# Inner attention's P ahead of the second half of its features, its rounded part first, and a new order of turns

## The reference

```
e = leaky_relu(s_i + t_j);  e = where(mask, e, -inf);  out_i = sum_j softmax_j(e)_ij * (h @ W)_j
```

## Time and profile before

| | us |
|---|---|
| median of the runs | 2882.01 |
| the profiled execution's own time | 2880.97 |
| its span, first to last instruction | 2879.2 |
| TensorE matmuls busy | 2827.2 (98%) |
| VectorE busy | 2551.1 (89%) |
| ScalarE busy | 2169.4 (75%) |
| GpSimd busy | 575.6 (20%) |
| mean granted TensorE clock | 0.996 |

### The profile page before, as it was taken

How to read it: one execution, slowest core, us unless ns; L and a number is a source line. 1 busy time by engine, 2 the same in 40 slices (tenths; PEclk the granted TensorE clock), 3 DMA queues, 4 the chain that set the end, 5 groups by cost and what they waited for, 6 DMA issues and landing times. The chain is left out here.

```text
span 2879.2 us, 66889 instructions
## 1 busy us (share of the span) xinstructions
PE 2827.2 (98%) x25368; PEld 2593.7 (90%) x25368; DVE 2551.1 (89%) x7305; ACT 2169.4 (75%) x5791; POOL 575.6 (20%) x731
## 2 busy tenths in 40 slices
PE   7999999999999999999999999999999999999998
PEld 7888998999999999998999999999989998999986
DVE  6898888998999899989988989889899888998977
ACT  5677778777777777787777787777777777777766
POOL 4021022211122211122211222111222111222001
PEclk8999999999999999999999999999999999999999
DMA  2000000000000000000000000000000000000000
GB/s 82 9 10 8 16 16 16 1 16 16 16 16 16 1 16 16 16 16 9 9 16 16 16 16 9 9 16 16 16 16 2 16 16 16 16 16 2 9 8 15
DMA packets 16800, 42.05 MB, mean 15 GB/s; under 512 B 5344, under 2 KB 7392, under 8 KB 16480
## 3 DMA queue, kind: packets, MB, share of 16 engines
q1 hardware_dynamic: 16480, 37.77, 3.7%
HBM read 20.99 MB, written 16.78 MB: 13 GB/s over the span
## 5 line engine op out<-in xcount | busy, mean ns | idle before, releaser
L690 PE MATMUL bank<-hw,R 128*128 128x257 f32 x3072 | 716.5, 381 | 4.4 <-DVE R L905 2.0
L690 PEld LDWEIGHTS bank<-hw,R 128*128 128x128 f32 x3072 | 562.2, 190 | 85.7 <-issue 11.1
L1380 POOL TENSOR_TENSOR rs<-ve,mhalf 128x4 f32<-128x4 f32 x128 | 133.5, 1043 | 1754.7 <-DVE ve L848 1649.5
L905 DVE SCALAR_TENSOR_TENSOR R<-bank,E,mask_ne 128x512 f32<-128x512 f32 x640 | 451.0, 741 | 19.1 <-PE bank L678 16.3
L592 PE MATMUL bank<-wfc_hi,oThi 128*128 128x256 f32 (+1 forms) x1024 | 302.5, 295 | 0.0
L592 PE MATMUL bank<-wfc_hi,oTlo 128*128 128x256 f32 (+1 forms) x1024 | 289.6, 283 | 0.0
L592 PE MATMUL bank<-wfc_lo,oThi 128*128 128x256 f32 (+1 forms) x1024 | 289.6, 283 | 0.0
L724 PEld LDWEIGHTS bank<-hw,R 128*64 128x64 f32 x8192 | 252.2, 139 | 29.3 <-issue 16.7
L724 PE MATMUL bank<-hw,R 128*64 128x65 f32 x8192 | 270.5, 225 | 6.6 <-DVE R L905 4.1
L1197 ACT ACTIVATE Z<-bank,rs 128x258 f32<-128x258 f32 (+1 forms) x384 | 177.8, 477 | 81.1 <-PE bank L592 80.8
L592 PEld LDWEIGHTS bank<-wfc_hi,oThi 128*128 128x128 f32 x1024 | 194.0, 189 | 1.7
(11 more groups left out here) (275 smaller groups left out, 8807.5 us busy)
## 6 DMA issues: line engine op xcount, KB each, us to landing
x<-in_x_dram SPq DMA_DIRECT2D x32, 512.0 KB, 3.5
out_dram<-x SPq DMA_DIRECT2D x31, 512.0 KB, 2.6
R<-in_adj_dram SPq DMA_DIRECT2D x2, 512.0 KB, 7.1
Z<-in_L_gnn_mlp_w_dram SPq DMA_DIRECT2D x2, 512.0 KB, 5.5
O<-in_L_gnn_W_fc_dram SPq DMA_DIRECT2D x1, 1024.0 KB, 6.8
out_dram<-x SPq DMA_DIRECT2D x4, 128.0 KB, 1.7
R<-in_L_gnn_W_dram SPq DMA_DIRECT2D x1, 256.0 KB, 3.8
R<-in_L_gnn_W_hand_dram SPq DMA_DIRECT2D x1, 256.0 KB, 6.6
```

The source lines that it names most:

```text
L690: ins = e.matmul(bk[:, 0:257], P[:, j, i * 128:(i + 1) * 128], hw[:, j, 0:257], start=(j == 0), stop=(j == NBLK - 1))
L905: e.scalar_tensor_tensor(P[:, t, :], bank_of(b, "row", p)[:, :], m["E"][:, 1, h, j:j + 1], mask[:, j, :], ALU.max, ALU.mult).then_inc(up(" ...
L1380: e.tensor_tensor(m["rs" + z][:, :], m["ve" + z][:, :], mhalf[:, :], ALU.pow).then_inc(up("rs", b), 1 if l == 1 else 3)
```

## The change

- VectorE: `low_part` gets a list of blocks. For HB it does block 0, then the four P tiles, then blocks 1 and 2, then the low part of P tile 0, then block 3, then the low parts of P tiles 1 to 3.
- ScalarE: rounded parts of HB's blocks 0 to 2, then P tile 0, then HB's block 3, then P tiles 1 to 3. Ahead of each rounded P stands a wait for the last hs2 turn, as the copy overwrites `oT`.
- TensorE's generator is unchanged.
- The strings for TensorE, VectorE, ScalarE and GpSimd are all new; SyncE's is as before. On GpSimd each batch's first turn (the root for layer 1's norm) now stands ahead of all 15 other turns of the batch before it, where it stood after the four of its first sums.

```diff
 TURNS = {
     "pe": (
...
-        "uttuutttuuuuuuttuvvtuuvvvuuuvuuvvvvuvvvvuvvtvvvvvvvvvvvvvvuuvvvuvuvvvvuuvvvvvvuvuvuvvvvuvvvvuuuuvvuvvvvvuuvvvv"
-        "vvvvuuuuvvuvvuvvuuuvuuuvuvvuvvvvvv"
...
+        "uuvvutttttutuutuuuvuvuvuvuuuvuuuuvvvvvuuvvuuvuuvuvuvuuuuuuuvvvvvvvvvuuvvvvvuuuvvvuvvuvuvvuuuuvvuvvvvuvuvuvvvvv"
+        "vvvvvvvvvvvvvvvvvvvvvvvvvvvvvvvvvv"
     ),
...
-            def low_part(kind, name):
+            def low_part(kind, name, ns=range(NBLK)):
                 H = HA if kind == "hA" else HB[s]
-                for n in range(NBLK):
+                for n in ns:
                     w.wait_ge(*at(kind, b, n))
...
             yield from scores(1, 1)
-            yield from low_part("hB", "hs2")
+            yield from low_part("hB", "hs2", (0,))
...
                                 ALU.mult, ALU.max).then_inc(up("P", b))
                 yield
+            yield from low_part("hB", "hs2", (1, 2))
             for j in range(NBLK):
+                if j == 1:
+                    yield from low_part("hB", "hs2", (3,))
                 w.wait_ge(*at("Phi", b, j))
...
-            for n in range(NBLK):
+            def high_hB(n):
                 w.wait_ge(*at("hs2", b, n))
                 e.copy(HB[s]["hi"][:, n, :], bank_of(b, "hs2", n)[:, 0:F]).then_inc(up("hB", b))
                 yield
+
+            for n in range(3):
+                yield from high_hB(n)
             for j in range(NBLK):
+                if j == 1:
+                    yield from high_hB(3)
+                w.wait_ge(*at("hs2", b, 3))
                 w.wait_ge(*at("P", b, 4, j))
                 e.copy(oT["hi"][:, j, :], R[s][:, j, :]).then_inc(up("Phi", b))
                 yield
```

More of the change, by code:

```diff
@@ L74 @@
[L74 to L88, removed]
@@ new lines @@
+        "33335444444544433554445443355444343535433444543433334444343554646554544454445556566644555444465454654444444555"
+        "55555655445566556446554455655455465544444455554546657576665565555566667776556655556565655575557566766667666667"
+        "76665577655565667656656576655555666656577686877676666667887777866777666676767686666668777777788776677787788667"
+        "76687787676677867766667777676887979878877787778889899977888777798787987777777888888889887788998897798877889887"
+        "8879887777778888787998a8a999889888889999aaa98899888898989888a888a899a9999a99999aa99988aa98889899a9899898a99888"
@@ new lines @@
+        "889999898aa9b9baa9a999999abbaaaab99aaa9999a9a9a9b999999baaaaaaabbaa99aaabaabb99aa99baaba9a99aab9aa9999aaaa9a9b"
+        "bacacbabbaaabaaabbbcbcccaabbbaaaacbabacbaaaaaaabbbbbbbbcbbaabbccbbcaacbbaabbcbbabbacbbaaaaaabbbbabaccbdbdcccbb"
+        "cbbbbbccccdddcbbccbbbbcbcbcbbbdbbbdbccdccccdcccccddcccbbddcbbbcbccdcbccbcbdccbbbbbccccbcbddceceddcdccccccdeedd"
+        "ddeccdddccccdcdcdceccccccedddddddeeddccdddeddeeccddcceddedcdccddecddccccddddcdceedfdfedeedddedddeeefefffddeeed"
+        "dddfededfedddddddeeeeeeeefeeddeeffeefddfeeddeefeedeedfeeddddddeeeededffegegfffeefeeeeeffffgggfeeffeeeefefefeee"
@@ new lines @@
+        "geeegeffgffffgfffffggfffeeggfeeefeffgfeffefegffeeeeeffffefeggfhfhggfgffffffghhgggghffgggffffgfgfgfhffffffhgggg"
+        "ggghhggffggghgghhffggffhgghgfgffgghfggffffggggfgfhhgigihghhggghggghhhihiiigghhhggggihghgihggggggghhhhhhhhihhgg"
+        "hhiihhiggihhgghhihhghhgihhgggggghhhhghgiihjhjiiihhihhhhhiiiijjjihhiihhhhihihihhhjhhhjhiijiiiijiiiiijjiiihhjjih"
+        "hhihiijihiihihjiihhhhhiiiihihjjikikjjijiiiiiijkkjjjjkiijjjiiiijijijikiiiiiikjjjjjjjkkjjiijjjkjjkkiijjiikjjkjij"
+        "iijjkijjiiiijjjjijikkjljlkjkkjjjkjjjkkklkllljjkkkjjjjlkjkjlkjjjjjjjkkkkkkkklkkjjkkllkkljjlkkjjkklkkjkkjlkkjjjj"
@@ new lines @@
+        "jjkkkkjkjllkmkmlllkklkkkkkllllmmmlkkllkkkklklklkkkmkkkmkllmllllmlllllmmlllkkmmlkkklkllmlkllklkmllkkkkkllllklkm"
+        "mlnlnmmlmllllllmnnmmmmnllmmmllllmlmlmlnllllllnmmmmmmmnnmmllmmmnmmnnllmmllnmmnmlmllmmnlmmllllmmmmlmlnnmomonmnnm"
+        "mmnmmmnnnonooommnnnmmmmonmnmonmmmmmmmnnnnnnnnonnmmnnoonnommonnmmnnonnmnnmonnmmmmmmnnnnmnmoonpnpooonnonnnnnoooo"
+        "ppponnoonnnnonononnnpnnnpnoopoooopoooooppooonnpponnnonooponoononpoonnnnnoooononppoqoqppopoooooopqqppppqoopppoo"
+        "oopopopoqooooooqpppppppqqppoopppqppqqooppooqppqpopooppqoppooooppppopoqqprprqpqqpppqpppqqqrqrrrppqqqpppprqpqpqp"
```

200 lines of the change are left out of this document (98 added, 102 removed).

## The result

The changed kernel takes 2905.38 us (median of 4 runs, 2902.43 to 2906.76); beside it the kernel before took 2879.97 (4 runs). The ratio is 1.0085 [1.0069, 1.0101]: 0.9% slower, clear of the scatter of the runs, and 4 us above the range of the prediction. The profiled execution has a span of 2902.8 us, 23.6 more than before.

The account below looks back on a forecast made before the run. TensorE's own work was taken to bound the middle, most idle time lying at the two ends. 2881.0 + 0 (edit) - 10 (middle) + 0 (head) + 10 (end) + 2 (clock) = 2883, 2884 on the median's scale; range 2866 to 2901 us.

Parts of the forecast that it names:

- The edit to P and the rounded parts: P's turns on VectorE and ScalarE: worth 0 to -1.9 us, ScalarE delay at most +12, taken as 0.
- Rival D: The change doesn't do what it says; edit and middle give 0, only the end counts, +12: 2894 us; chance 0.12.
- The new order, middle: Middle batches: -10 us, 87.0 us a batch, out of at most 23 us to win.
- 261 or less: Sign of being right: three batches of the middle pass in 261 us or less.
- no new tight place: Middle, TensorE's work between dependent turns: top to row and row to first attend keep 1.4 us or more.
- Rival C: First layer's packed heads: VectorE overruns 0.5 us a batch, +13, 2907 us; sign over 1 us idle a batch; chance 0.07.
- The new order, head: Loads and first batch's chain fix most of TensorE's 14.9 us idle: 0, bounds -5 to +5 us.
- The new order, end: Last batches: lone end of batch 31 costs +17.3, stretch ahead gains -7; together +10 us, bounds +7 and +17.
- The clock: Lone end: one fall of TensorE's clock to half speed, +2 us in the sum.
- The chain of links: Batch 31's last 39 TensorE turns alone, summed from dependent steps: 56.0 us, one layer 20.6; sign 54 to 60.
- rival B: Last 56 us: clock falls to half repeatedly, +9 for +2, 2896 us; sign over 10 of last 60 us; chance 0.14.
- The step ahead of it: Stretch before the lone end: batch 30's layers fill batch 31's waits, -7 us, bounds -10.4 and 0.

Follow-up runs that it names:

- e4: Changed kernel with only the edit to P undone, turns of P moved back on VectorE and ScalarE: 2955.09 us, 1.0261 of the kernel before.
- e5: Kernel before with the edit to P alone, in batches 0 to 25, old order otherwise: 2915.23 us, 1.0127 of the kernel before.
- e14: Changed kernel with GpSimd's second group of row sums, at full size, started later in batches 3 to 27: 2910.06 us, 1.0102 of the kernel before.
- e1: Kernel before with the new order up to the end of batch 2 and the edit in batches 0 to 3: 2875.92 us, 0.999 of the kernel before.
- e12: The same kernel as e1, measured again over 11 runs: 2876.76 us, 0.9979 of the kernel before.
- e3: Kernel before up to 2566 us of its trace, then the new order to the end: 2893.2 us, 1.0043 of the kernel before.
- e8: Changed kernel with filler matmuls on TensorE in the waits of batch 31's last two layers, results unchanged: 2899.77 us, 1.0072 of the kernel before.
- e10: Changed kernel with VectorE's turn for top4 two places earlier in its string: 2910.67 us, 1.01 of the kernel before.
- e11: Changed kernel with VectorE's turn for top4 three places earlier in its string: 2920.3 us, 1.0131 of the kernel before.

## Why the prediction was wrong, step by step

**"The edit to P and the rounded parts", 0: wrong in its reason.** The wait for P's low parts is gone, as predicted, and in this order the edit does no harm: without it the order is 50 us slower (e4). But I bounded its price by ScalarE's wait and TensorE's own wait, at 0 to +12, and left out what stands behind the four P tiles on VectorE. e5 priced that at +34 us in the old order. Rival D ("does nothing") was wrong for the same reason.

**"The new order, middle", -10: this is the step that failed.** It came to +19.5 in the trace, 88.06 instead of 87.0 us a batch. Three batches took 263.9 us, not the 261 or less that I had named as the sign of being right. That sign was itself set too low: the 261.4 us of the earlier trace rows hold all attends of three batches but 2356 matmul records, and from mark to mark it is 2374 records in 261.9 us. The changed kernel, then the kernel before:

```profile
1343.20:1607.10 263.90, 261.53 (x2374) 240.44 (x2370) 237.97 (x683) 203.87 (x541) 51.80 (x66) 1.00 0.04 13
...
1341.80:1603.70 261.90, 260.86 (x2374) 240.23 (x2368) 236.67 (x682) 201.80 (x541) 53.23 (x66) 1.00 0.04 14
```

I saw "no new tight place" because I counted TensorE's work between dependent turns and not what VectorE has to do in the same time. Rival C counted that, found 21 of 23 us and priced an overrun at 0.5 us a batch; I gave it 0.07, on the strength of an average of 89% busy. Place and sign were C's: the waits lie at m2 and top4. The loss was 0.74 us a batch and not 0.5, with 0.84 us of TensorE's idle time a batch where C's sign asked for over 1. And C's reason was only part of it. It took VectorE's durations as constants from their groups' means; with short sums, where they nearly are, the orders differ by 0.18 (87.02 against 86.84), and the other 0.56 is the stretch beside GpSimd, which no rival had.

The Trainium skill, "SBUF — State Buffer", section "Who interferes with whom", says that VectorE and GpSimd share a pair of ports under an exclusive lock: a VectorE instruction with two inputs in SBUF contends with a GpSimd instruction that reads SBUF, and one with at most one such input, outside the two-port modes, does not. The rows above agree: L967, L969 and, in the kernel before, L1034, with two inputs in SBUF, are stretched (0.42 to 1.44, 0.42 to 0.85, 0.68 to 1.81 us), and L905 and L1029, with one input in PSUM, are not (0.74, 0.67). The 1.44 ends 0.29 us after GpSimd's first sum does. That sum is longer itself, 1.67 us where e14's takes 1.30, and it started while L1033 ran. The prediction had GpSimd at 20% and passed it over; a share of 20% cost VectorE 22.2 us of 1585.0, because it lay at the wrong operations.

**"The new order, head", 0 (-5 to +5): right in size.** -3 to -6 by e1 and e12; the -10.7 of the traces holds some us of falls of the clock, which differ between executions (e3, whose head is the old one, passed the first mark at 289.5 and not 293.7), and 1.4 us of one m2 turn that the new order puts behind the mark.

**"The new order, end", +10, and "The clock", +2: sum nearly right, in part by luck, and the clock too small.** Predicted +12, measured +12.3 (e3) to +14.8 (traces). The chain of links was nearly right: the 39 turns without the last division and store, 56.0 - 4.25 = 51.75 us, took 53.2 in e8 at nearly full clock (0.97). The sum has a hole: the projection's link ends at 2859.0 to 2859.1 and the next begins at 2859.75, and these 0.7 us, in two layers, are 1.4. By parts the last layer nevertheless took 20.75 us in e8 for the 20.6 of the sum, and the distance lies in the one before (25.0 for 23.3). At the granted clock of the changed kernel they took 58.8, with the last division and store 63.1, outside the 54 to 60 that I had named. The granted clock was 0.50 (1.2 GHz) in four stretches of the last 62.8 us, 10.2 + 6.8 + 3.4 + 6.8 = 27 us, behind idle time of TensorE in batch 31's chain (busy 7.1 of the 10 us before the first). That is rival B's mechanism, which I gave 0.14, and its sign, over 10 us at half in the last 60, was there: it costs 5.6 us, and the +2 was 4 short of it. There were four falls where the forecast had one. The chain that ended last shows it in batch 31's layer 2 (start, us, what): an attend of 7.85 us took

```profile
2865.12 9.44 PE bank L690 x32
```

The step ahead of it went better than the -7, near its bound: from the mark of batch 29 to the lone end it took 264.8 us (2574.9 to 2839.7), before 274.6 (to 2840.5), -9.8, and in 2747.6 to 2840.0 TensorE was idle 3.5 us where the earlier trace rows had 10.4. The lone end cost 63.1 - 38.7 = +24.4 for the +19.3 of links and clock. These two errors of 3 and 5 us partly cancel.

By the traces, on the scale of the spans, the 21.6 us between forecast and result are: middle +29.5 (from -10 to +19.5), head -10.7, end and clock together +2.8 (14.8 for 12). The range left rival C out, and so it ended 4 us too low.

## What to carry to other kernels

When an order of turns is packed anew, count for each short stretch what every engine must do in it, not only the one that is busiest on average; and count two engines that get in each other's way as one there. A list of waits tells where the wait came out, not what would be won: e10 and e11 removed the wait at the head of the list, e14 halved it, and none won anything, while cutting the work of an engine that is 20% busy brought 17 us in a kernel whose list named it nowhere. And two orders can be compared by stretch only between marks that enclose the same work: marks that leave four m2 turns out of one order would make the loss of 0.74 us a batch look like 1.00. The new order's head on the old order's middle beats both kernels, the one before by 0.2%: 0.9979 [0.9969, 0.9989].
